# Two-layer graph network on one core: a gather ring of 35 groups instead of 11 in layer 0, and the accumulator cleared in two halves between the layers

## The chip, the cores and the metric

The kernel runs on one core of a Trainium2 chip. The metric is the time of one execution on the device in microseconds (us); three executions were timed, and one more was profiled. TensorE, VectorE, ScalarE, GpSimd and SyncE are the core's engines; the profile calls them PE (PEld is TensorE's weight load), DVE, ACT, POOL and SP.

## What is computed

6250 nodes with 128 features, 106250 edges sorted by their destination, 4 edge types. Two layers, each on the normalized features of the one before and added to them:

```python
h = max(layernorm(x), 0)
x = x + segment_sum((h @ W.T + b)[src] * edge_weight[:, None], dst)      # layer 0

h = max(layernorm(x), 0)
msgs = 0
for t in range(4):                                                      # layer 1
    m = relu(concat(h[src], h[dst]) @ W1[t] + b1[t]) @ W2[t] + b2[t]
    msgs = msgs + where(edge_type == t, m, 0)
agg = segment_sum(msgs, dst)
x = x + gru_cell(agg, h)
```

## The kernel before

Edges are taken in tiles of 128 and in groups of `GT` = 4 tiles; there are `NGRP` = 208 groups and 50 chunks of 125 nodes (`NCH`, `CW`). After a prologue (loads, first layernorm, `h @ W.T + b` for all nodes, stored as `h0_tab`) each engine runs its own loop for layer 0 (`f0_pool`, `f0_act`, `f0_pe`, `f0_dve`, `f0_sp`) and then for layer 1 (`f1_...`). The order on each engine is the order in which these loops are written; engines meet only at semaphores.

Layer 0, for group g:

- GpSimd (`f0_pool`, line 1164) issues four indirect DMAs, each of which gathers the 128 source rows of one tile from `h0_tab` into a slot of a ring, `slot0(g % R0)`. The ring has `R0` = 11 slots of 4 x 132 columns of the array `accs`. From group 11 on it waits until `out0` is at least g - R0 + 1, that is, until TensorE has done with the group that was in the slot.
- ScalarE (`f0_act`, `weigh`, line 1253) waits for the four transfers and multiplies each row by its edge weight in place. It is 4 groups ahead of the step of the loop.
- VectorE (`f0_dve`, `hots`, lines 1182 and 1183) writes the one-hot matrices of the edge's node in the chunk and of its type. It is 6 groups ahead, in a ring of `HR` = 8, and waits for `out0` of at least g - 7.
- TensorE (`f0_pe`, `group`, line 1311) multiplies the two and sums two groups into a PSUM bank; eight passes are recorded per group. It counts up `out0`.
- VectorE (`gather_sums`, line 1223) adds the finished sums of two groups to the nodes in `xs`, after a wait for `out0` of at least 2(o + 1) for pair o.

For each chunk c whose sums are complete, some groups later: VectorE computes the layernorm (`variance`, `normalize`, lines 1191 to 1207), TensorE transposes it (`turned`, lines 1319 and 1320), ScalarE applies the relu (`hidden`, line 1268), TensorE multiplies with the two halves of `W1` (lines 1326 and 1333), ScalarE and VectorE copy the results out (`p_out`, line 1274; `q_out`, line 1212), and SyncE stores them as `p_tab` and `q_tab` (lines 1355 and 1357). `st` has one place for each, so `q_out` waits for the store before.

Layer 1 uses the same array `accs` (25088 columns) as its accumulator and needs it zero. Its lower half (12544 columns, up to `A0`) holds the one-hot ring and the gather ring in layer 0, its upper half only prologue data. So ScalarE clears the upper half in 50 pieces, one after each `p_out` (`clear`, line 1278), two unused pieces at step 0, and, when all groups are done, the rest in 12 pieces (`zero`, line 1247). VectorE waits for `zeroed` = R0 + 3 and `c_zero` = 50 before its first accumulation of layer 1.

At the start of layer 1, GpSimd (line 1369) gathers from `p_tab` as soon as all groups of layer 0 and all stores of `p_tab` are done, into a ring of 12 groups. VectorE writes three one-hot matrices (`hots`, line 1411), TensorE transposes them (line 1520), ScalarE copies the transposes (`hot_copy`, line 1473), TensorE expands the rows of `q_tab` (line 1529), VectorE adds the gathered rows (`total`, line 1419, which frees a slot), ScalarE applies the relu (line 1477), TensorE sums (line 1539), VectorE accumulates (line 1464).

Of the kernel before, what the change touches and what calls it, by code (L numbers as in the profile page):

```python
# [27 lines left out]
ACT = mybir.ActivationFunctionType  # L28
AX = mybir.AxisListType.X

P = 128
WIN = 32
GT = 4
# [4 lines left out]
CW = 125  # L38
# [6 lines left out]
def gnn_program(nc, x, src, dst, etype, eweight, W0, b0, W1, b1, W2, b2, Wih, Whh, bih, bhh, out):  # L45
    N, D = x.shape
    E = src.shape[0]
    T = W1.shape[0]
    KEYS = WIN * T
    NCH = N // CW  # L50
# [4 lines left out]
    PB = NT // PR // NBLK  # L55
    NCOL = NT + UT
    NW = -(-N // WIN)
    NPAD = NW * WIN
# [16 lines left out]
    with ExitStack() as ctx:  # L75
        def sb(name, shape, dt=F32):
            return ctx.enter_context(nc.sbuf_tensor(name, shape, dt))
# [5 lines left out]
        accs = sb("accs", [P, NPAD * T])  # L83
        acc0 = accs[:, 0:NPAD]
        cnt = accs[0:T + 1, NPAD:2 * NPAD]
        A0 = 2 * NPAD
# [28 lines left out]
        nought = sb("nought", [P, 1])  # L115
# [47 lines left out]
        LIN = NCH * D  # L163
        x_rows = accs[0:CW, 0:LIN].rearrange("p (c d) -> p c d", d=D)
        TG = [(c, min(4, NCH - c)) for c in range(0, NCH, 4)]
# [11 lines left out]
        g_cnt = cntb[:, 0, :]  # L177

        NGRP = NT // GT
        R0, R1 = 11, 12  # L180
        FW = D + T
        HR = 8
        NOCT = NT // (NBLK * PR)
        GO = NGRP // NOCT
        F0 = LIN
        assert NOCT == PB and F0 + R0 * GT * FW <= A0 and F0 + (len(TG) - 1) * 4 * D <= A0 and HR * GT * CW <= LIN
        from_t = nodehot[0:CW, :, :, :].rearrange("p a b n -> p (a b n)")[:, 0:NOCT]
        next_t = nodehot[0:CW, :, :, :].rearrange("p a b n -> p (a b n)")[:, NOCT:2 * NOCT]

# [6 lines left out]
        def slot1(k):  # L196
# [33 lines left out]

            "mid_d mid_a mid_p st_c st_h st_p st_q upd_d upd_a upd_p upd_ld upd_st "

            "iota_set c_var c_sqrt c_nrm c_hT c_h1 c_p c_pe c_q c_qe c_zero "

            "u_agg u_aggc u_gate u_rz u_pre u_tanh u_new u_out u_add").split()}
        s_x = [sem(f"s_x{i}") for i in range(NPC)]
# [414 lines left out]
        def h0_stored(eng):  # L651
            eng.wait_ge(s["tab"], 32 * len(TG))
# [517 lines left out]
        def f0_dve(eng):  # L1170
# [38 lines left out]
            def q_out(c):  # L1209
                eng.wait_ge(s["c_q"], c + 1)  # L1210
                eng.wait_ge(s["st_q"], c * 16 + 16)
                eng.tensor_tensor(st[0:CW, 2, :], pb[5][0:CW, :], b1r[0:CW, :], ALU.add).then_inc(s["c_qe"], 1)
# [13 lines left out]
            for g in range(-SEEN0, STEPS0):  # L1226
                if g + SEEN0 < NGRP:
                    hots(g + SEEN0)
                o = (g - GO) // GO
                if (g - GO) % GO == 0 and 0 <= o < NOCT:  # L1230
                    if o % 4 == 0:
                        first = bases(eng, NT // PR + o, 4, NCH - 1)
                    gather_sums(o, first[o % 4])
                if (c := chunk_at(g, D_NRM)) is not None:
                    normalize(c)
                if (c := chunk_at(g, D_STATS)) is not None:
                    variance(c)
                if (c := chunk_at(g, D_Q)) is not None:
                    q_out(c)

        def f0_act(eng):
            h0_stored(eng)
            eng.wait_ge(s["preT"], 6)
            ZW = -(-(NPAD * T - A0) // NCH)

            def zero(ap):
                eng.activation(ap, nought[0:ap.shape[0], :].to_broadcast([ap.shape[0], ap.shape[1]]), ACT.Copy).then_inc(s["zeroed"], 1)

            def weigh(g):
                G0 = slot0(g % R0)  # L1250
                eng.wait_ge(s_g0[g % R0], 16 * GT * (g // R0 + 1))
                for t in range(GT):
                    ins = eng.activation(G0[:, t, 0:D], G0[:, t, 0:D], ACT.Copy, scale=w_t[:, g * GT + t:g * GT + t + 1])  # L1253
                ins.then_inc(s["dv0"], 1)

            def root(c):
                eng.wait_ge(s["c_var"], c + 1)
                if c >= 2:
                    eng.wait_ge(s["c_nrm"], c - 1)
                eng.activation(sd2[0:CW, c % 2, :], mv2[0:CW, c % 2, 1:2], ACT.Sqrt).then_inc(s["c_sqrt"], 1)  # L1260

            def hidden(c):
                eng.wait_ge(s["c_hT"], c + 1)
                if c >= 2:
                    eng.wait_ge(s["c_q"], c - 1)
                eng.wait_ge(s["st_h"], max(c, 1) * 16)
                eng.wait_ge(s["st_c"], max(c, 1) * 16)
                eng.activation(h1b[:, c % 2, :], pb[4][:, 0:CW], ACT.Relu, scale=2.0)  # L1268
                eng.activation(cntb[0:T, c % 2, :], pb[4][0:T, 128:128 + CW], ACT.Copy).then_inc(s["c_h1"], 1)

            def p_out(c):
                eng.wait_ge(s["c_p"], c + 1)
                eng.wait_ge(s["st_p"], c * 16 + 16)
                eng.activation(st[0:CW, 1, :], pb[7][0:CW, :], ACT.Copy).then_inc(s["c_pe"], 1)

            def clear(c):
                part_c = accs[:, A0 + c * ZW:min(A0 + (c + 1) * ZW, NPAD * T)]
                eng.activation(part_c, nought[:, :].to_broadcast([P, part_c.shape[1]]), ACT.Copy).then_inc(s["c_zero"], 1)

            for g in range(-WEIGHED0, STEPS0):  # L1280
                if g + WEIGHED0 < NGRP:
                    weigh(g + WEIGHED0)
                if (c := chunk_at(g, A_HID)) is not None:
                    hidden(c)
                if (c := chunk_at(g, A_ROOT)) is not None:
                    root(c)
                if (c := chunk_at(g, A_P)) is not None:
                    p_out(c)
                    clear(c)
                if g == 0:  # L1290
                    zero(accs[:, HR * GT * CW:LIN])
                    zero(accs[:, F0 + R0 * GT * FW:A0])
            eng.wait_ge(s["out0"], NGRP)
            zero(accs[:, 0:HR * GT * CW])
            for k in range(R0):
                zero(accs[:, F0 + k * GT * FW:F0 + (k + 1) * GT * FW])

        def f0_pe(eng):
            eng.wait_ge(s["preC"], 6)
# [104 lines left out]
        def f1_dve(eng):  # L1404
# [37 lines left out]
            for g in range(-3, STEPS1):  # L1442
                if g + 3 < NGRP:
                    hots(g + 3)
                if 0 <= g + 1 < NGRP:
                    total(g + 1)
                if (c := chunk_at(g, 4)) is not None:
                    add_x(c)
                if (c := chunk_at(g, 2)) is not None:
                    candidate(c)  # L1450
                if (c := chunk_at(g, 3)) is not None:
                    blend(c)
                if 0 <= g < NGRP:
                    if g == 0:
                        eng.wait_ge(s["zeroed"], R0 + 3)
                        eng.wait_ge(s["c_zero"], NCH)
                    if g % NG == 0:
                        base = bases(eng, g * GP, NG * GP)
                    eng.wait_ge(s["out1"], g + 1)
                    for p in range(GP):  # L1460
                        if g or p:
                            eng.wait_ge(s["acc1"], g * GP + p)
                        a = accs[:, bass.ds(base[g % NG * GP + p] * T, KEYS)]
                        eng.tensor_tensor(a, pb[4 + g % 2][:, p * KEYS:(p + 1) * KEYS], a, ALU.add).then_inc(s["acc1"], 1)  # L1464
# [228 lines left out]
```

## Time and profile before

| | us |
|---|---|
| median of 3 executions | 2747.63 (2742.65 to 2761.39) |
| the profiled execution | 2750.62 |
| its span | 2748.6 |
| first and last gather of layer 0 issued | 67.6 and 1259.5 |
| last `q_out` of layer 0 | 1300.8 |
| GpSimd busy | 1592.7 (58%) |
| TensorE busy | 1388.9 (51%) |
| VectorE busy | 799.1 (29%) |
| ScalarE busy | 637.3 (23%) |

The span is the profiled execution as its instructions show it; 2 us lie around it. Issuing an indirect DMA counts as busy time of GpSimd. No engine is busy for two thirds of the span, so the time is in who waits for whom.

### The profile page before, as it was taken

The numbers are of one execution on the slowest core, as the hardware profiler recorded it, in microseconds if no ns is written. First come the engines' busy times: TensorE is split into PE (matmuls) and PEld (weight loads), VectorE is DVE, ScalarE is ACT, GpSimd is POOL, SyncE is SP. The second block draws the span as 40 slices with busy tenths as digits, with TensorE's granted clock in tenths as the row PEclk, the third lists the DMA queues.
The fourth block names the chain that finished last, engine by engine and source line by source line (L and its number), as shares of the span: only waits on it lengthen the run. The fifth ranks groups of instructions, "written<-read, shape, count | busy, mean of one in ns | idle before, by whom it ended". The sixth has DMA issues, their size and how long they took to land.

```text
span 2748.6 us, 25831 instructions
## 1 busy us (share of the span) xinstructions
PE 1388.9 (51%) x7484; PEld 1186.3 (43%) x7484; DVE 799.1 (29%) x2307; ACT 637.3 (23%) x1773; POOL 1592.7 (58%) x1697
## 2 busy tenths in 40 slices
PE   4233444344344444444146555665655656666666
PEld 3222333233233323332145555555555655555556
DVE  6112222222222222223023233333323333333333
ACT  4212222222222222223011212121212122122122
POOL 2756666666666666662755555555555555555550
PEclk9556666566566656666578888888888798888889
DMA  8212222222222222222222222222222222222220
GB/s 190 53 40 54 75 70 73 67 72 75 68 70 76 71 67 69 79 71 77 66 58 60 61 69 58 67 60 67 62 67 60 67 68 62 68 61 67 63 66 24
DMA packets 160437, 186.49 MB, mean 68 GB/s; under 512 B 50285, under 2 KB 118728, under 8 KB 159919
## 3 DMA queue, kind: packets, MB, share of 16 engines
q0 software_dynamic: 53248, 109.16, 15.9%
q1 hardware_dynamic: 105802, 74.84, 9.8%
q8 instruction: 64, 1.05, 0.2%
q10 hardware_dynamic: 1244, 0.79, 0.1%
q14 instruction: 79, 0.65, 0.1%
HBM read 149.29 MB, written 35.35 MB: 67 GB/s over the span
## 4 chain that ended last, share of the span: by engine, by line
another core or an unknown queue 37%; PE 24%; issue 19%; DVE 13%; ACT 2%; SPq 2%; DVEq 2%; DMA 1%; POOL 0%; ACTq 0%
PE bank L1539 6%; PE bank L1529 5%; PE bank L1311 4%; PE bank L1520 4%; DVE hot L1411 2%; DVE accs L1464 2%; DVE accs L1183 2%; DVE xs L1223 1%; DVE rows L1419 1%; SPq L313 1%; ACT hotT L1473 1%; PE bank L1552 1%; DMA q_tab<-st 1%; DVEq L701 1%
## 5 line engine op out<-in xcount | busy, mean ns | idle before, releaser
L1164 POOL DMA_INDIRECT accs<-h_tab,src_t x832 | 787.4, 946 | 433.8 <-issue 239.5
L1311 PE MATMUL bank<-accs 128*125 128x132 f32 x1664 | 374.7, 360 | 414.8 <-issue 387.6
L1311 PEld LDWEIGHTS bank<-accs 128*125 128x125 f32 x1664 | 329.8, 264 | 518.6 <-issue 499.1
L1520 PE MATMUL bank<-ident,hot 128*128 128x128 f32 x832 | 166.5, 334 | 597.7 <-DVE hot L1411 388.5
L1369 POOL DMA_INDIRECT G<-p_tab,src_t x288 | 272.4, 946 | 259.1 <-DVE rows L1419 129.6
L1464 DVE TENSOR_TENSOR accs<-bank,accs 128x128 f32 x416 | 121.3, 292 | 924.3 <-remote 376.6
L1520 PEld LDWEIGHTS bank<-ident,hot 128*128 128x128 f32 x832 | 107.6, 166 | 637.1 <-DVE hot L1411 409.1
L1369 POOL DMA_INDIRECT edge<-p_tab,src_t x272 | 257.3, 946 | 190.5 <-DVE rows L1419 106.4
L1529 PE MATMUL bank<-qwin,hotT 128*128 128x128 f32 x1664 | 288.7, 331 | 0.9 <-ACT hotT L1473 0.9
L1253 ACT ACTIVATE accs<-accs,edge 128x128 f32<-128x128 f32 x832 | 258.2, 387 | 96.7 <-DMA accs<-h_tab,src_t 96.7
L1539 PE MATMUL bank<-hot,rows 128*128 128x128 f32 x1664 | 272.8, 318 | 1.2 <-ACT rows L1477 1.2
L1529 PEld LDWEIGHTS bank<-qwin,hotT 128*128 128x128 f32 x1664 | 269.7, 245 | 1.0 <-ACT hotT L1473 1.0
L1539 PEld LDWEIGHTS bank<-hot,rows 128*128 128x128 f32 x1664 | 259.6, 237 | 1.6 <-ACT rows L1477 1.6
L1223 DVE SCALAR_TENSOR_TENSOR xs<-bank,nodehot,xs 125x132 f32 x208 | 64.0, 349 | 455.7 <-remote 309.8
L1473 ACT ACTIVATE hotT<-bank 128x512 f32<-128x512 f32 x208 | 123.8, 595 | 283.4 <-PE bank L1520 165.8
L1369 POOL DMA_INDIRECT g_more<-p_tab,src_t x136 | 128.6, 946 | 77.5 <-issue 44.3
L1319 PE MATMUL bank<-ident,st 125*128 125x125 f32 x50 | 21.1, 421 | 290.7 <-DVE st L1207 191.2
L1268 ACT ACTIVATE h1b<-bank 128x125 f32<-128x125 f32 x50 | 13.8, 276 | 642.7 <-remote 519.7
L1182 DVE TENSOR_TENSOR accs<-bank,edge 128x16 f32<-128x16 f32 x208 | 36.5, 176 | 420.8 <-remote 334.2
L1483 ACT ACTIVATE st<-bank 128x125 f32<-128x125 f32 x50 | 13.9, 277 | 583.6 <-remote 312.7
L1319 PEld LDWEIGHTS bank<-ident,st 125*128 125x128 f32 x50 | 8.5, 170 | 309.3 <-DVE st L1207 205.8
L1411 DVE TENSOR_TENSOR hot<-bank,key_t 128x512 f32<-128x512 f32 x208 | 141.4, 681 | 0.1
(158 smaller groups left out, 1734.0 us busy)
## 6 DMA issues: line engine op xcount, KB each, us to landing
qwin<-q_tab SPq DMA_DIRECT2D x416, 64.0 KB
accs<-h_tab,src_t POOLq DMA_INDIRECT x832
q_tab<-st SPq DMA_DIRECT2D x50, 250.0 KB
p_tab<-st SPq DMA_DIRECT2D x49, 250.0 KB
G<-p_tab,src_t POOLq DMA_INDIRECT x288
edge<-p_tab,src_t POOLq DMA_INDIRECT x272
h_tab<-h1b SPq DMA_DIRECT2D x50, 62.5 KB
h1b<-h_tab SPq DMA_DIRECT2D x50, 62.5 KB
```

Of the source, the lines that this page charges most:

```text
L1164: eng.indirect_dma_start(slot0(g % R0)[:, t, 0:D], None, h0_tab, bass.IndirectOffsetOnAxis(src_t[:, k:k + 1], 0)).then_inc(s_g0[g % R0], 16)
L1183: eng.tensor_tensor(ones_of(g % HR), mid(iota_p[:, 0:CW], GT), bcast(rel_t[:, cols], CW), ALU.is_equal).then_inc(s["hot0"], 1)
L1223: ins = eng.scalar_tensor_tensor(a, got, m[:, o:o + 1], a, ALU.mult, ALU.add)
L1253: ins = eng.activation(G0[:, t, 0:D], G0[:, t, 0:D], ACT.Copy, scale=w_t[:, g * GT + t:g * GT + t + 1])
L1311: ins = eng.matmul(pb[SUM_BANK[o % 4]][0:CW, 0:FW], ones_of(g % HR)[:, t, :], slot0(g % R0)[:, t, :], start=n == 0, stop=n == GO * GT - 1)
L1369: eng.indirect_dma_start(slot1(g % R1)[:, t, :], None, p_rows, bass.IndirectOffsetOnAxis(src4_t[:, k:k + 1], 0)).then_inc(s_g1[g % R1], 16)
L1411: eng.tensor_tensor(hot[:, g % NG], mid(iota_p, GT), bcast(key_t[:, g * GT:(g + 1) * GT], KEYS), ALU.is_equal).then_inc(s["hot1"], 1)
L1464: eng.tensor_tensor(a, pb[4 + g % 2][:, p * KEYS:(p + 1) * KEYS], a, ALU.add).then_inc(s["acc1"], 1)
L1473: eng.activation(hotT[:, g % 2, :], pb[0][:, :], ACT.Copy).then_inc(s["tc1"], 1)
L1520: ins = eng.transpose(pb[0][:, t * P:(t + 1) * P], hot[:, g % NG, t, :], ident[:, :])
L1529: ins = eng.matmul(pb[2 + g % 2][:, t * D:(t + 1) * D], hotT[:, g % 2, t * P:(t + 1) * P], qwin[:, g % NG, t // PR, :], start=True, stop=True)
L1539: ins = eng.matmul(pb[4 + g % 2][:, p * KEYS:(p + 1) * KEYS], rows[:, g % 2, t, :], hot[:, g % NG, t, :], start=t % PR == 0, stop=t % PR = ...
```

## The change

The ring of layer 0 becomes 35 slots. It begins where it began (`F0` = 6400) and now ends at column 24880, in the upper half of `accs`. The 50 clears within layer 0 and the 14 other clears of ScalarE go. In their place VectorE clears the upper half in one memset after its last `q_out`, and ScalarE the lower half in one activation after `out0` = 208. `zeroed` is now waited for at 2. The number of gather semaphores follows R0.

```diff
-        R0, R1 = 11, 12
+        R0, R1 = 35, 12
...
-        assert NOCT == PB and F0 + R0 * GT * FW <= A0 and ...
+        assert NOCT == PB and F0 + R0 * GT * FW <= NPAD * T and ...
...
                 if (c := chunk_at(g, D_Q)) is not None:
                     q_out(c)
+            eng.memset(accs[:, A0:], 0.0).then_inc(s["zeroed"], 1)
...
                 if (c := chunk_at(g, A_P)) is not None:
                     p_out(c)
-                    clear(c)
-                if g == 0:
-                    zero(accs[:, HR * GT * CW:LIN])
-                    zero(accs[:, F0 + R0 * GT * FW:A0])
             eng.wait_ge(s["out0"], NGRP)
-            zero(accs[:, 0:HR * GT * CW])
-            for k in range(R0):
-                zero(accs[:, F0 + k * GT * FW:F0 + (k + 1) * GT * FW])
+            eng.activation(accs[:, 0:A0], nought[:, :].to_broadcast([P, A0]), ACT.Copy).then_inc(s["zeroed"], 1)
...
                     if g == 0:
-                        eng.wait_ge(s["zeroed"], R0 + 3)
-                        eng.wait_ge(s["c_zero"], NCH)
+                        eng.wait_ge(s["zeroed"], 2)
```

On GpSimd, at the start of layer 0 (`h_tab` is the gathered table, `s_out0` TensorE's count of finished groups), before:

```order
L678 COMPARE_AND_BRANCH
L1590 UNCONDITIONAL_BRANCH
L1164 DMA accs<-h_tab,src_t 128x128 [waits s_preC,s_preT,s_tab]
L1164 DMA accs<-h_tab,src_t 128x128 x43
L1164 DMA accs<-h_tab,src_t 128x128 [waits s_out0]
L1164 DMA accs<-h_tab,src_t 128x128 x3
```

and now:

```order
L678 COMPARE_AND_BRANCH
L1575 UNCONDITIONAL_BRANCH
L1164 DMA accs<-h_tab,src_t 128x128 [waits s_preC,s_preT,s_tab]
L1164 DMA accs<-h_tab,src_t 128x128 x139
L1164 DMA accs<-h_tab,src_t 128x128 [waits s_out0]
L1164 DMA accs<-h_tab,src_t 128x128 x3
```

The first wait for TensorE stands ahead of gather 141 instead of 45 (counted from 1).

On ScalarE, at the end of layer 0 (`nought` is the zero that is copied), before:

```order
L1274 ACTIVATE st<-bank 125x512 [waits s_st_p,s_c_p]
L1278 ACTIVATE accs<-nought 128x245
L1247 ACTIVATE accs<-nought 128x4000 [waits s_out0]
L1247 ACTIVATE accs<-nought 128x528 x11
L1467 ACT_TABLE_LOAD
L1467 ACTIVATE tiny<-tiny 128x1
L1473 ACTIVATE hotT<-bank 128x512 [waits s_tr1] x2
```

and now:

```order
L1270 ACTIVATE st<-bank 125x512 [waits s_st_p,s_c_p] x2
L1282 ACTIVATE accs<-nought 128x12544 [waits s_out0]
L1452 ACT_TABLE_LOAD
L1452 ACTIVATE tiny<-tiny 128x1
L1458 ACTIVATE hotT<-bank 128x512 [waits s_tr1] x2
```

Twelve clears ahead of the table load have become one, of 12544 columns in place of 9808.

On VectorE, at the same place, before:

```order
L1207 TENSOR_SCALAR st<-xs,mv,rs 125x128 [waits s_c_hT,s_step]
L1212 TENSOR_TENSOR st<-bank,b1r 125x512 [waits s_st_q,s_c_q] x3
L561 TENSOR_TENSOR brz<-bg 128x2 [waits s_sets,s_tab]
L1411 TENSOR_TENSOR hot<-bank,key_t 128x512 x3
L1419 TENSOR_TENSOR rows<-bank,G 128x512 [waits s_gather1_0,s_exp1]
```

and now:

```order
L1207 TENSOR_SCALAR st<-xs,mv,rs 125x128 [waits s_c_hT,s_step]
L1212 TENSOR_TENSOR st<-bank,b1r 125x512 [waits s_st_q,s_c_q] x3
L1240 MEMSET accs 128x12544
L561 TENSOR_TENSOR brz<-bg 128x2 [waits s_sets,s_tab]
L1397 TENSOR_TENSOR hot<-bank,key_t 128x512 x3
L1405 TENSOR_TENSOR rows<-bank,G 128x512 [waits s_gather1_0,s_exp1]
```

The memset stands between the last `q_out` of layer 0 and the first one-hot matrices of layer 1.

## Rows read from the trace of the kernel before

**Rows 1.** The page's groups: busy, mean ns of one | idle time before, releaser.

```profile
L1164 POOL DMA_INDIRECT accs<-h_tab,src_t x832 | 787.4, 946 | 433.8 <-issue 239.5
```

**Rows 2.** Lines 1164 and 1253 until 330 us, 1164 after it; 1253 in the page.

```profile
L1164 POOL DMA_INDIRECT accs<-h_tab,src_t x186: 942/947/1183, 67.6 to 329.5; - x186
...
L1164 POOL DMA_INDIRECT accs<-h_tab,src_t x647: 942/947/973, 329.5 to 1259.5; - x162
...
  remote: 114.3, 37
  PE bank L1311: 20.7, 7
...
L1253 ACT ACTIVATE accs<-accs,edge 128x128 f32<-128x128 f32 x832 | 258.2, 387 | 96.7 <-DMA accs<-h_tab,src_t 96.7
...
L1253 ACT ACTIVATE accs<-accs,edge x176: 384/386/402, 74.2 to 327.5; 128x128 f32<-128x128 f32 x176
...
  DMA accs<-h_tab,src_t: 96.7, 21
```

**Rows 3.** Timeline, 104 to 180 us: start, us, engine, what, [idle before <-releaser].

```profile
116.50 0.62 DVE L1223 SCALAR_TENSOR_TENSOR xs<-bank,nodehot,xs 125x132 f32 x2 [21.86 <-remote]
...
126.19 0.38 PE L1311 MATMUL bank<-accs 128*125 128x132 f32 x1 [2.41 <-issue]
...
138.87 0.17 DVE L1182 TENSOR_TENSOR accs<-bank,edge 128x16 f32<-128x16 f32 x1 [21.08 <-remote]
...
157.81 7.00 PE L1311 MATMUL bank<-accs 128*125 128x132 f32 x38 [0.35 <-issue]
157.91 0.62 DVE L1223 SCALAR_TENSOR_TENSOR xs<-bank,nodehot,xs 125x132 f32 x2 [18.28 <-remote]
158.03 0.95 POOL L1164 DMA_INDIRECT accs<-h_tab,src_t  x1 [10.43 <-remote]
```

**Rows 4.** Timeline of GpSimd in the middle of layer 0.

```profile
333.28 0.94 POOL L1164 DMA_INDIRECT accs<-h_tab,src_t  x1 [0.30 <-issue]
...
347.04 0.94 POOL L1164 DMA_INDIRECT accs<-h_tab,src_t  x1 [4.06 <-remote]
...
375.84 0.95 POOL L1164 DMA_INDIRECT accs<-h_tab,src_t  x1 [4.08 <-PE bank L1311]
...
1032.61 0.95 POOL L1164 DMA_INDIRECT accs<-h_tab,src_t  x1 [3.99 <-remote]
```

**Rows 5.** Timeline of GpSimd and VectorE at the start of layer 1.

```profile
1302.57 0.95 POOL L1369 DMA_INDIRECT G<-p_tab,src_t  x1 [42.12 <-DMA p_tab<-st]
...
1381.54 0.29 DVE L1464 TENSOR_TENSOR accs<-bank,accs 128x128 f32 x1 [43.62 <-remote]
...
1383.74 0.95 POOL L1369 DMA_INDIRECT G<-p_tab,src_t  x1 [11.45 <-DVE rows L1419]
```

**Rows 6.** End of layer 0: line 1311 in a stretch (PE and PEld busy, passes), line 1212.

```profile
1259.50 0.95 POOL L1164 DMA_INDIRECT accs<-h_tab,src_t  x1 [0.31 <-issue]
...
1262.70:1277.60 14.90, 9.09 (x64) 8.98 (x64) 0.81 0.25 76
...
L1212 DVE TENSOR_TENSOR st<-bank,b1r x7: 681/692/692, 1264.9 to 1300.8; 125x512 f32<-125x512 f32 x7
```

**Rows 7.** Timeline: memsets of the prologue, ScalarE and VectorE between the layers; two forms.

```profile
3.23 0.91 DVE L487 MEMSET accs<- 8x1024 int32 x1 [0.16 <-issue]
4.31 0.91 DVE L488 MEMSET accs<- 8x1024 f32 x1 [0.16 <-issue]
...
L1247 ACT ACTIVATE accs<-nought 128x528 f32<-128x528 f32 x11 | 5.9, 628 | 0.0
...
L1247 ACT ACTIVATE accs<-nought 128x4000 f32<-128x4000 f32 x1 | 3.5, 3526 | 0.0
...
1298.01 9.37 ACT L1247 ACTIVATE accs<-nought 128x4000 f32<-128x4000 f32 x12
...
1308.80 0.58 ACT L1473 ACTIVATE hotT<-bank 128x512 f32<-128x512 f32 x1
...
1312.53 0.69 DVE L1419 TENSOR_TENSOR rows<-bank,G 128x512 f32<-128x512 f32 x1 [9.13 <-issue]
```

More of the change, by code:

```diff
@@ L185, in gnn_program @@
         F0 = LIN
-        assert NOCT == PB and F0 + R0 * GT * FW <= A0 and F0 + (len(TG) - 1) * 4 * D <= A0 and HR * GT * CW <= LIN
+        assert NOCT == PB and F0 + R0 * GT * FW <= NPAD * T and F0 + (len(TG) - 1) * 4 * D <= A0 and HR * GT * CW <= LIN
         from_t = nodehot[0:CW, :, :, :].rearrange("p a b n -> p (a b n)")[:, 0:NOCT]
@@ L231, in gnn_program @@
             "mid_d mid_a mid_p st_c st_h st_p st_q upd_d upd_a upd_p upd_ld upd_st "
-            "iota_set c_var c_sqrt c_nrm c_hT c_h1 c_p c_pe c_q c_qe c_zero "
+            "iota_set c_var c_sqrt c_nrm c_hT c_h1 c_p c_pe c_q c_qe "
             "u_agg u_aggc u_gate u_rz u_pre u_tanh u_new u_out u_add").split()}
@@ L1243, in f0_act @@
             eng.wait_ge(s["preT"], 6)
-            ZW = -(-(NPAD * T - A0) // NCH)
-            def zero(ap):
-                eng.activation(ap, nought[0:ap.shape[0], :].to_broadcast([ap.shape[0], ap.shape[1]]), ACT.Copy).then_inc(s["zeroed"], 1)
             def weigh(g):
@@ L1274, in p_out @@
                 eng.activation(st[0:CW, 1, :], pb[7][0:CW, :], ACT.Copy).then_inc(s["c_pe"], 1)
-            def clear(c):
-                part_c = accs[:, A0 + c * ZW:min(A0 + (c + 1) * ZW, NPAD * T)]
-                eng.activation(part_c, nought[:, :].to_broadcast([P, part_c.shape[1]]), ACT.Copy).then_inc(s["c_zero"], 1)
             for g in range(-WEIGHED0, STEPS0):
```

## The prediction

> **What bounds the kernel now.** I read the groups of the page first, for who waits in layer 0. GpSimd is the busiest engine there: 832 gathers of 946 ns, and 433.8 us idle in front of them [rows 1]. That looks like a gather-bound layer whose ring is too short. So I next asked what ended those waits, and where. Between 330 and 1262 us (647 gathers) 37 waits of 114.3 us ended by a "remote" semaphore and 7 of 20.7 us by TensorE, 135.0 us together [rows 2]. In this stretch that can only be the ring wait on `out0` (the rest, "issue", is the 0.30 us between two gathers). A ring that is full means that the producer is ahead. The other side says the same: ScalarE, which takes each group when it has landed, waited for gathers 96.7 us in the whole run, and all 96.7 us lie before 330 us [rows 2]. After that every group had landed when it was asked for. The consumers set the pace, and a gather issued earlier helps nobody at that moment.
>
> Why do the consumers crawl, when TensorE does eight groups in 14.9 us once the gathers have ended [rows 6]? The timeline of the first gathers answers [rows 3]. GpSimd issues without a pause from 67.6 (rows 2) to 147.6 us (158.03 - 10.43). VectorE waits for `out0` = 4 until 116.50, for 5 (21.08 us of it in one wait) until 138.87 and for 6 until 157.91 (wait values read from `hots` and `gather_sums`): 22.4 us, then 19.0 us, for a group of eight passes, 2.8 us per pass, though the passes are issued no earlier than their data is there and nothing else is waited for ("issue"). Then, 10.4 us after the last gather of the run was issued, everything moves: TensorE does 38 passes in 7.0 us and the ring opens (GpSimd [10.43 <-remote]). The same happens at the start of layer 1: gathers run from 1302.6 to 1372.3 (1383.74 - 11.45), VectorE waits 43.62 us until 1381.54, and the ring opens after 11.45 us [rows 5]. In the steady state it is a short cycle: 20 gathers, then a stop of 4 us until TensorE's count arrives. It was 4.06 us at 347.04, 4.08 us at 375.84 (28.8 us later, so a run of 24.7 us, which is 20 gathers of 1.25) and 3.99 us at 1032.61 [rows 4]. I read this as a coupling: while gathers are issued back to back, TensorE's completions trickle, and a pause of the gathers releases them. About 38 passes (nearly five groups) of backlog are released at each pause, and that is why the cycle is five groups in 28.8 us, 5.76 us per group. What the coupling consists of the profile does not show.
>
> **The trace against a rule.** By rows 3 and 5 TensorE's counts arrive only when GpSimd's gathers pause. The Trainium skill ("SBUF — State Buffer", section "Who interferes with whom") says the opposite: TensorE and ScalarE have their own ports, never wait on anyone, and a DMA never contends with a compute engine. By that rule the slow passes are TensorE's own and a longer uninterrupted run of gathers costs nothing. What it would make of the time is rival B, worked out there from rows. The trace does not agree so far; it does not exclude it either, as no stretch without gathers and with the same work lies before 1260 us.
>
> **The change, part by part.** The sum is made on the profiled execution (2750.62 us, span 2748.6); the median of the runs shown, 2747.63, is 3.0 us lower, which is taken off at the end.
>
> (a) *GpSimd's head start.* With 35 slots the first ring wait stands before gather 141 instead of 45, and it passes if `out0` is 1. A gather costs 0.947 + 0.30 = 1.25 us, a group 5.01 us. At TensorE's 22.4 us per group, `out0` is 5 at 138.9 and grows by one each 22.4 us. Group 47 needs `out0` = 13, due near 318 us, while GpSimd would be there at 67.6 + 47 x 5.01 = 303.1 us; group 46 needs 12 at 298.1, which is just there. So the first full ring comes at group 47 at 303 us, and ends with the release after about 11 us (10.43 and 11.45 are the two releases after long runs), at 314 us. Before, group 47 was issued at 333.28 us [rows 4] (gather 186 at 329.5, rows 2). Gain: **-19 us**. Bounds: if the release grows with the run (10.43 us after 80 us, so 0.13 x 235 = 31 us), nothing is gained, 0; if TensorE trickles at 11.5 us per group, as it does inside the short cycles, the ring fills near group 58 and the gain is about -33 us.
>
> (b) *The remaining 161 groups.* One slot is freed per group in either kernel, so the ring is full as before and the cycle of 20 gathers and a 4 us stop stays: 0 us. GpSimd's last gather ended at 1259.5 + 0.95 = 1260.4 us [rows 6] and now ends at 1241 us.
>
> (c) *The backlog at the end.* When GpSimd ends its last gather, TensorE is a ring behind: about 34 groups in place of 10, 24 more. They are worked off without gathers beside them. The rate: 64 passes, eight groups, in 14.9 us, 1.86 us a group; and the last seven `q_out` stand 35.9 / 6 = 5.98 us apart, 1.50 us per group, set by the store of `q_tab` before each [rows 6]. Between these I take 1.7 us: **+41 us** (bounds +36 and +45). Thus (a) and (c) put the end of layer 0, which was the end of the last `q_out` at 1300.8 + 0.7 = 1301.5, at 1301.5 - 19 + 41 = 1324 us.
>
> (d) *The clears.* VectorE's new memset of 12544 columns lies behind its last `q_out` and ahead of layer 1's first `hots`. The four prologue memsets of 1024 columns start 1.07 us apart [rows 7], so it takes 12544 x 1.07 / 1024 = 13.1 us. ScalarE's last clears took 9.37 us for 9808 columns; one of 12544 takes, by the 4000-column row (3.53 us, 0.83 ns a column above the fixed part), 10.7 us, +1.3 us, and stays hidden behind VectorE's. The first `total` of layer 1 was at 1312.53, after ScalarE's clears and table load (first copy at 1308.80) [rows 7]. Now it is 13.1 us of memset plus about 5 us of hots, transposes, copy and expansion after 1301.5, so 1319.6: 7 us later against the start of the layer. But GpSimd's gathers start at once, and the ring of 12 fills 60 us later, with TensorE trickling meanwhile; its release decides when work moves, and there group 14 waits for `total(2)`. I count about one handshake, **+3 us** (bounds 0 and +13, the whole memset). The 50 clears of 0.4 us inside layer 0 lay in ScalarE's waits; their removal counts 0.
>
> Sum: -19 + 0 + 41 + 3 = +25 us, 2775.6 us profiled, **2772 us** as a median. That is 0.9% over before; about 1% is what a measurement of this kernel can tell from no change, so the forecast is "same, at its slow edge". With the bounds of (a), (c) and (d), half of each taken, its own range is 2755 to 2792.
>
> **The rivals.**
> - *A, the release grows with the run (slower).* One mechanism: the pause that frees TensorE is proportional to the gathers issued before it. For it: 10.43 us after 80 us, 4.06 after 24.7. Against it: 11.45 us after only 70 us [rows 4, 5], which looks like a fixed backlog. It decides once a run is over some 150 us. The first stop costs 31 us instead of 11, (a) is 0: 2747.6 + 0 + 41 + 3 = 2792 us.
> - *B, no coupling (same).* TensorE is slow by itself and the gathers are innocent. For it: the passes are also spaced out in places where ScalarE and VectorE idle; against it: the release a constant 4 us after each stop, and fast passes everywhere after 1262. Then `out0` = 208 comes at 1277.6 as before, the gathers merely wait in the slots, and only (d) with 3 to 13 us remains: 2755 us.
> - *C, the ring was the bound (faster).* GpSimd never stops: 67.6 + 208 x 5.01 = 1110 us, the tail of 41 us behind it gives 1151 instead of 1301.6, minus 151 us, plus 3: 2600 us. For it: the 135 us of ring waits; against it: not one wait of ScalarE for a gather after 330 us.
> - *D, the memset holds up the first gathers of layer 1.* It begins at the moment at which GpSimd issues them (1302.57, rows 5). If they queue behind it, layer 1 starts 12 us later on top: 2784 us. For it: no memset of VectorE lies beside a gather in the trace, so nothing excludes it; against it: of 647 gathers beside VectorE's other work none took over 0.973 us, where the median is 0.947 [rows 2].
>
> **How the numbers follow.** Forecast 0.50, A 0.17, B 0.20, C 0.06, D 0.07. Slower by over 1% (above 2775): all of A, most of D and about 0.2 of the forecast, 0.43. Faster by over 1%: C and a little of a lucky start, 0.08. Within 1%: 0.49. The range reaches down past B to 2742 and up past A, whose backlog could drain at 1.86 us a group, to 2805.
>
> **What would show it.** Right: GpSimd issues some 188 gathers without a stop, until about 303 us; the first stop is 10 to 12 us; then the cycle of 20 gathers and 4 us; the last gather near 1241 us; 40 us more between it and the end of layer 0; TensorE's `out0` waits on VectorE of 22 us until after 300 us. The memset 13.1 us, and the first `total` 18 us after the last `q_out`. Wrong: a first stop of 30 us (A); TensorE keeping its old pace with gathers long finished and a full set of slots (B); gathers ending near 1110 us and the layer with them (C); the first gather of layer 1 held back behind the memset (D). If TensorE completes groups at less than 11 us each during the long first run, the step from rows 3 fails.

## The result and the profile after

| | before | changed |
|---|---|---|
| median of the timed runs, us | 2750.53 (4 runs, 2742.65 to 2761.39) | 2783.62 (4 runs, 2769.98 to 2796.91) |
| ratio to before, 95% interval | 1 | 1.0109 (1.0059 to 1.0159) |
| profiled execution, us (span) | 2750.62 (2748.6) | 2779.37 (2777.3) |

The changed kernel is slower by 1.1%, 30 us (0.6 to 1.6%; the two medians are 33 us apart). The interval lies wholly above a ratio of 1, but the difference is small, and the runs of the two kernels spread over 19 and 27 us. The forecast was 2772 us, +0.9%. In the changed kernel the gather stays at line 1164; ScalarE's weighing is line 1249, the group's passes line 1297, the memset line 1240, ScalarE's one clear line 1282, the gathers of layer 1 line 1355 and their sums line 1405.

The page and the view of the gather's line, to be held against [rows 1, 2] (idle time before, and what ended it):

```profile
span 2777.3 us, 25768 instructions
...
L1164 POOL DMA_INDIRECT accs<-h_tab,src_t x832 | 787.2, 946 | 425.6 <-issue 241.6
```

```profile
L1164 POOL DMA_INDIRECT accs<-h_tab,src_t x832: 938/944/1237, 68.8 to 1251.8; - x167
...
  remote: 124.6, 32
  PE bank L1297: 30.6, 10
...
  ACT accs L1249: 78.9, 18
```

The ring waits are still there: 155 us in 42 waits, against 166 us in 51 before. ("remote" is a wait whose end has no record in the trace; at this line only TensorE's count `out0` can end one.) Tripling the ring removed next to nothing of them, because the ring fills once and then opens at the consumers' pace. ScalarE waits 78.9 us for gathers (96.7 before), so the producer is still ahead.

Now the first stretch, from timelines of the changed kernel (start, us, engine, what, [idle before <-releaser]). PE is TensorE's matmul, PEld its weight load. First TensorE alone, then VectorE alone:

```profile
91.76 2.10 PE L1297 MATMUL bank<-accs 128*125 128x132 f32 x8 [2.90 <-issue]
...
106.73 2.09 PE L1297 MATMUL bank<-accs 128*125 128x132 f32 x8 [2.87 <-issue]
111.67 1.65 PE L1297 MATMUL bank<-accs 128*125 128x132 f32 x6 [2.84 <-issue]
114.60 0.38 PE L1297 MATMUL bank<-accs 128*125 128x132 f32 x1 [1.28 <-issue]
```

```profile
92.90 0.17 DVE L1182 TENSOR_TENSOR accs<-bank,edge 128x16 f32<-128x16 f32 x1 [7.64 <-remote]
...
115.98 0.17 DVE L1182 TENSOR_TENSOR accs<-bank,edge 128x16 f32<-128x16 f32 x1
...
137.75 0.17 DVE L1182 TENSOR_TENSOR accs<-bank,edge 128x16 f32<-128x16 f32 x1 [21.03 <-issue]
```

For the first 44 us of gathers TensorE is not slow: from 76.96 to 113 us it starts eight passes in 2.1 us, one group each 5 us, as fast as the gathers bring them. What is late is its count. VectorE's three operations above wait for `out0` = 3, 4 and 5. The last passes of these groups end by the record (ends are modelled) at 88.9, 93.9 and 98.9 us, and the operations start 4, 22 and 39 us later. For the eighth group the delay is 87 us, and there it stays up to the 13th: about four groups are run and not yet counted. Only when the delay has grown this far, from 113 us on, do the passes themselves start late. The other three traces with these times (before, e11, e12) show the same in the same order. In short, "TensorE creeps" below means: a count of `out0` each 22.4 us, and from 113 us on a pass each 2.8 us.

Then rows from the stretch up to the release, from timelines of all engines:

```profile
204.23 0.29 PEld L1297 LDWEIGHTS bank<-accs 128*125 128x125 f32 x1 [2.51 <-issue]
...
206.33 0.38 PE L1297 MATMUL bank<-accs 128*125 128x132 f32 x1 [3.12 <-issue]
...
208.43 0.28 PEld L1297 LDWEIGHTS bank<-accs 128*125 128x125 f32 x1 [3.91 <-issue]
209.14 0.38 PE L1297 MATMUL bank<-accs 128*125 128x132 f32 x1 [2.43 <-issue]
...
210.54 0.28 PEld L1297 LDWEIGHTS bank<-accs 128*125 128x125 f32 x1 [1.83 <-issue]
...
211.93 0.38 PE L1297 MATMUL bank<-accs 128*125 128x132 f32 x1 [2.41 <-issue]
...
316.48 0.94 POOL L1164 DMA_INDIRECT accs<-h_tab,src_t  x1 [10.21 <-remote]
...
318.33 0.38 PE L1297 MATMUL bank<-accs 128*125 128x132 f32 x1 [3.12 <-issue]
...
335.37 0.94 POOL L1164 DMA_INDIRECT accs<-h_tab,src_t  x1 [14.21 <-remote]
...
342.86 3.27 PE L1297 MATMUL bank<-accs 128*125 128x132 f32 x12 [0.32 <-issue]
343.82 0.94 POOL L1164 DMA_INDIRECT accs<-h_tab,src_t  x1 [3.76 <-remote]
```

GpSimd ran from 68.8 us almost without a stop to 306.3 us (316.48 - 10.21): 188 gathers, as forecast. From 113 us on a weight load and its matmul started mostly 1.4 or 2.1 us apart, 2.8 us per pass, as in [rows 3]. The `hots` of VectorE, which wait for one count each, start at 181.8, 204.9, 226.6, 249.7, 271.4, 294.5 and 316.2 us: 22.4 us each. But the stop of 10.2 us brought no release; at 318 us TensorE still crept. GpSimd got one slot, did one group, stopped for 14.2 us, did one more, stopped for 3.8 us, and only then (342.86: twelve passes in 3.27 us) was TensorE free. So TensorE crept for 37 us in which GpSimd issued only eight gathers. From 384 us on the old cycle runs: gathers for 24.7 us, a stop of 4.0 us.

The end of layer 0 and the start of layer 1 in the changed kernel: the last `q_out` additions in the view of line 1212, then the timeline.

```profile
L1212 DVE TENSOR_TENSOR st<-bank,b1r x50: 679/683/692, 399.5 to 1328.0; 125x512 f32<-125x512 f32 x50
```

```profile
1326.04 10.65 ACT L1282 ACTIVATE accs<-nought 128x12544 f32<-128x12544 f32 x1
...
1327.99 0.69 DVE L1212 TENSOR_TENSOR st<-bank,b1r 125x512 f32<-125x512 f32 x1 [4.03 <-DMA q_tab<-st]
...
1329.73 0.94 POOL L1355 DMA_INDIRECT G<-p_tab,src_t  x1 [77.01 <-DMA p_tab<-st]
1330.98 0.94 POOL L1355 DMA_INDIRECT G<-p_tab,src_t  x1 [0.30 <-issue]
1331.25 10.51 DVE L1240 MEMSET accs<- 128x12544 f32 x1 [2.56 <-issue]
...
1341.69 1.88 DVE L1397 TENSOR_TENSOR hot<-bank,key_t 128x512 f32<-128x512 f32 x3
...
1351.43 0.69 DVE L1405 TENSOR_TENSOR rows<-bank,G 128x512 f32<-128x512 f32 x1 [7.86 <-remote]
...
1410.62 0.94 POOL L1355 DMA_INDIRECT G<-p_tab,src_t  x1 [11.29 <-DVE rows L1405]
```

GpSimd's one long wait between the layers, 42.12 us in [rows 5], is now 77.01 us. This is the loss. The stages of the two profiled executions side by side, in us:

| | before | changed | difference |
|---|---|---|---|
| last gather of layer 0 ends | 1260.4 | 1252.7 | -7.7 |
| first gather of layer 1 starts | 1302.6 | 1329.7 | +27.2 |
| last gather of layer 1 starts | 2673.7 | 2701.4 | +27.7 |
| span | 2748.6 | 2777.3 | +28.7 |

The head start is worth 7.7 us, the longer backlog costs 34.9 us, and what comes after it (the clears among it) 0.5 us up to the last gather and 1.0 us more behind it. The backlog can be counted: when GpSimd's last gather of layer 0 ended, TensorE had started the passes of 200 of the 208 groups before, and of 176 now. These 24 groups are the 24 added slots. They arise in the first run: at 347 us, with GpSimd at group 49 in either kernel, TensorE had started 42 groups before and 20 now. They are worked off fast, with no gathers beside them; the view of line 1297 up to 1300 us:

```profile
L1297 PE MATMUL bank<-accs x221: 274/276/428, 1258.8 to 1300.0; 128*125 128x132 f32 x111
```

221 passes in 41.2 us are 1.5 us per group.

### The profile page after: what moved, and what is told of

It is laid out like the page before. It is cut to its first block, busy times and chain, and to the rows that moved or that the text cites. A ratio compares the mean times of both kernels' runs of the same rounds, so it can differ in the third digit from the quotient of the medians.

```text
span 2777.3 us, 25768 instructions
## 1 busy us (share of the span) xinstructions
PE 1370.3 (49%) x7484; PEld 1172.8 (42%) x7484; DVE 808.2 (29%) x2308; ACT 619.9 (22%) x1710; POOL 1590.4 (57%) x1697
## 4 chain that ended last, share of the span: by engine, by line
another core or an unknown queue 40%; PE 23%; issue 17%; DVE 12%; ACT 3%; SPq 2%; DMA 2%; DVEq 1%; ACTq 0%
PE bank L1514 5%; PE bank L1524 5%; PE bank L1297 4%; PE bank L1505 4%; DVE hot L1397 2%; DVE accs L1449 2%; DVE accs L1183 2%; DVE rows L1405 1%; ACT accs L1249 1%; DVE xs L1223 1%; SPq L313 1%; PE bank L1537 1%; ACT hotT L1458 1%; DMA q_tab<-st 1%
## 5 line engine op out<-in xcount | busy, mean ns | idle before, releaser
L1297 PE MATMUL bank<-accs 128*125 128x132 f32 x1664 | 364.7, 350 | 491.0 <-issue 466.9
L1297 PEld LDWEIGHTS bank<-accs 128*125 128x125 f32 x1664 | 319.9, 254 | 594.3 <-issue 582.3
L1249 ACT ACTIVATE accs<-accs,edge 128x128 f32<-128x128 f32 x832 | 257.9, 387 | 78.9 <-DMA accs<-h_tab,src_t 78.9
L1183 DVE TENSOR_TENSOR accs<-bank,edge 128x500 f32<-128x500 f32 x208 | 139.2, 669 | 0.0
```

What stands on the lines that cost most here:

```text
L1183: eng.tensor_tensor(ones_of(g % HR), mid(iota_p[:, 0:CW], GT), bcast(rel_t[:, cols], CW), ALU.is_equal).then_inc(s["hot0"], 1)
L1297: ins = eng.matmul(pb[SUM_BANK[o % 4]][0:CW, 0:FW], ones_of(g % HR)[:, t, :], slot0(g % R0)[:, t, :], start=n == 0, stop=n == GO * GT - 1)
```

## The experiments

One fact has to be known to read them. The first ten runs fell on chips (two of them) on which the kernel before takes about 2200 us, not 2750: one fifth less for the same program. The last two fell on a chip of the 2750 us kind. "Kind" says only this; whether it is the chip or a state that it was in, no run shows. Each run stands beside the kernel before, on its own chip, so the ratios are sound, but they answer for that kind of chip.

**e1_clears_only**: the changed kernel, with the ring put back.

```diff
-        R0, R1 = 35, 12
+        R0, R1 = 11, 12
```

> The new clears alone, with the old ring of 11. My theory (gathers issued back to back hold up TensorE's completions; the long ring costs 24 more groups of backlog, the clears almost nothing): 0 to +4 us against the kernel before (ratio 1.000 to 1.0015), layer 0's last q_out near 1301 us as before, the first total of layer 1 some 20 us after it, but the last gather of layer 1 within 3 us of before. Rival (the clears cost it: the memset of 13.1 us stands on the path at the start of layer 1): +13 us or more, ratio 1.005 and up.

Measured: 2201.42 us against 2201.23, ratio 0.9999 (0.999 to 1.0008). The gathers end at 1107 us and never wait for the ring. The clears cost nothing, here.

**e2_slots35_waits11**: the changed kernel, 35 slots, but GpSimd waits as if there were 11.

```diff
-                if g >= R0:
-                    eng.wait_ge(s["out0"], g - R0 + 1)
+                if g >= 11:
+                    eng.wait_ge(s["out0"], g - 11 + 1)
```

> 35 slots, but the gather of group g waits for out0 of g - 10 as with 11 slots; everything else as changed. My theory: what counts is how far GpSimd may run ahead, not where the slots lie: the same as e1_clears_only within 3 us, first stop of the gathers at group 16 near 148 us, cycle of 20 gathers and 4 us. Rival (the cost comes with the slots themselves, their place in the array or the number of semaphores): like the changed kernel, +25 to +35 us.

Measured: 2200.8 us, ratio 1.0 (0.9991 to 1.0009). As no gather waits for the ring on this kind of chip, this does not tell how far GpSimd may run ahead from the slots themselves, and the run was not made on the other kind.

**e3_ring23**: the changed kernel with 23 slots (`R0, R1 = 23, 12`).

> Ring of 23, half way. My theory: the first stop comes at group 31 near 223 us, 10 us of head start are won over the kernel before, 12 more groups of backlog at 1.5 to 1.7 us cost 18 to 20 us: +10 to +15 us in all, half of the changed kernel's. Rival (a threshold: a ring above some size is slow at once, or a cost of the clears): the same as the changed kernel, +25 us or more; or 0.

Measured: 2199.75 us, ratio 0.9996 (0.9987 to 1.0005). Nothing costs anything on this chip, the ring neither. The reason is plain in the profile of e5, below.

**e4_gathers_stop_at_35**: the changed kernel, in which the gathers of groups 35 to 207 of layer 0 are left out; those groups are computed on the rows that lie in the slots. It no longer computes the layer; it shows what the consumers can do with no gathers beside them.

```diff
-            for g in range(NGRP):
-                if g >= R0:
-                    eng.wait_ge(s["out0"], g - R0 + 1)
+            for g in range(R0):
...
-                eng.wait_ge(s_g0[g % R0], 16 * GT * (g // R0 + 1))
+                eng.wait_ge(s_g0[g % R0], 16 * GT)
```

> The changed kernel, in which GpSimd gathers only the first 35 groups of layer 0 and all later groups work on what then lies in the slots (the gathers of 173 groups are left out). It tells the coupling from rival B. My theory: from the last gather near 245 us plus about 10 us on, TensorE's counts come at once and the consumers do a group in 1.5 to 1.9 us: layer 0's last q_out near 255 + 200 x 1.6 + 24 = 570 to 650 us. Rival B (TensorE is slow by itself, 5.7 us per group whether gathers run or not): layer 0 still ends near 1300 us.

Measured: 1593.86 us (one run). A row of the view of stretches (stretch, length, then busy time of PE, PEld, DVE, ACT and POOL, granted clock, DMA share, GB/s):

```profile
260.00:400.00 140.00, 133.12 (x878) 105.49 (x877) 131.74 (x463) 132.03 (x468) 0.00 (x0) 1.00 0.31 97
```

738 of the 878 passes are those of the groups (the others belong to the chunks), 92 groups in 140 us, with TensorE, VectorE and ScalarE all over 90% busy and the granted clock at its full 2.4 GHz: 1.5 us per group. The last `q_out` starts at 531 us, ahead of the 570 to 650 expected. The consumers need a third of GpSimd's 5.0 us per group. This is a chip of the 2200 us kind, so the run does not decide against rival B for the other; there the 1.5 us per group after the last gather, shown above, says the same of the work itself.

**e5_changed_again**: the changed kernel, unaltered, on a second chip of the 2200 us kind.

> The changed kernel once more. On the chip of the last four runs the kernel before took 2201 us instead of 2750, and its gathers never stopped. My theory now has a condition: the long ring costs only where TensorE's completions trickle while gathers run. So where the kernel before takes about 2200 us, this one is the same within 3 us (ratio 0.999 to 1.002), layer 0's last gather at 1107 us; where it takes about 2750 us, the ratio is 1.008 to 1.014 again. Rival (the change is slower by its instructions alone): 1.005 or more in both.

Measured: 2203.3 us against 2203.8, ratio 0.9994 (0.9984 to 1.0003). The view of the gather's line there:

```profile
L1164 POOL DMA_INDIRECT accs<-h_tab,src_t x832: 941/946/1181, 68.1 to 1108.0; - x167
...
  issue: 243.3, 798
...
  PE bank L1297: 10.1, 33
...
  ACT accs L1249: 752.0, 163
```

and its timeline at the place where the 2750 us chip shows a pass each 2.8 us:

```profile
206.12 1.75 PE L1297 MATMUL bank<-accs 128*125 128x132 f32 x8 [2.98 <-issue]
...
211.15 2.09 PE L1297 MATMUL bank<-accs 128*125 128x132 f32 x8 [3.28 <-ACT accs L1249]
```

The gathers themselves are as fast (946 ns, 0.30 us apart). But eight passes take 1.75 us, not 22.4, and each count of `out0` is seen within 2 us of the group's last pass. GpSimd never stops, ScalarE waits 752 us for gathers, and the layer is bound by the gathers' issue. It is the picture that rival C drew, with its number (last gather near 1110 us), but with either ring: on such a chip 11 slots are more than enough, and 35 change nothing.

**e6_pause_after_gathers**: the kernel before, with a memset of 128 columns on GpSimd, waited for, after each gather of layer 0.

```diff
+                    pool_seq(eng, eng.memset(rest[:, :], 0.0))
```

> The kernel before (ring 11), with a GpSimd memset of 128 columns, and a wait for it, after each gather of layer 0: 0.2 to 0.4 us more per gather, so 1.5 to 1.65 us instead of 1.25. Where gathers never stop (2200 us), the layer is as long as its gathers: 832 x 0.3 = +170 to +330 us. Where TensorE's completions trickle (2750 us), my theory is that the back-to-back issue is what holds them up: spaced gathers free them and the stops of 4 us vanish, so the layer grows by no more than 832 x 1.6 - 1193 = +140 us and may even be unchanged. Rival (TensorE slow by itself there): stops stay, time unchanged within 5 us.

Measured: 2372.98 us, ratio 1.0764 (1.0743 to 1.0786). The gathers come each 1.44 us and end at 1281.7. The 169 us more are 832 gathers at 0.2 us each, just below the range that was expected. Without the trouble, pauses are pure loss. Whether they would pay on the other kind was not tried.

**e7_packets_ring11** and **e8_packets_ring35**: the kernel before and the changed one, with small loads added to each chunk, to see whether crowded DMA engines make TensorE creep.

```diff
+                for i in range(2):
+                    if c:
+                        eng.wait_ge(s_rest[i], 16 * c)
+                    with nc.allow_non_contiguous_dma(reason="small packets"):
+                        eng.dma_start(rest[:, i, :, 0:8], h0_tab[i * P:(i + 1) * P, :].rearrange("p (a b) -> p a b", b=8)).then_inc(s_rest[i], 16)
```

> The kernel before, with two extra loads per chunk in layer 0, each of 2048 descriptors of 32 bytes, into a scratch tile that nothing reads, issued by SyncE. It asks whether a stream of small packets can bring about the trickle of TensorE's completions on a chip where the kernel before takes 2201 us. My theory (too many small packets in flight hold up TensorE's completions): GpSimd shows ring waits, TensorE's passes spread to over 1 us with nothing waited for, the layer gets over 50 us longer. Rival (the trickle belongs to the chip on which the first runs were made and packets do not matter): layer 0 ends within 15 us of 1137 us, no ring waits.

> The same extra loads in the changed kernel (ring of 35). If the packets bring the trickle about: slower than e7_packets_ring11 by 10 to 30 us, as the backlog at the end of the gathers is 24 groups larger. If they only slow the gathers or nothing: the same as e7_packets_ring11 within 4 us. If the longer ring absorbs late gathers (my rival C): faster than e7.

Measured: 2206.29 us, ratio 1.0026 (1.0014 to 1.0038), and 2204.88 us, 1.0027 (1.0015 to 1.0039), with 366838 packets in place of 160437. Over twice the packets, no ring wait and no late count: on this kind of chip such packets don't bring the trickle about. The same on a chip that has it was not run.

**e9_slow_consumer_ring11** and **e10_slow_consumer_ring35**: the kernel before and the changed one, with 48 redundant products per pair of groups, so that TensorE is slow by its own work at any time, gathers or not.

```diff
+                for i in range(48 if g % GO == 0 else 0):
+                    eng.matmul(pb[SUM_BANK[o % 4]][0:CW, 0:FW], ones_of(g % HR)[:, i % GT, :], slot0(g % R0)[:, i % GT, :],
+                               start=True, stop=True)
```

> The kernel before with 48 additional products per pair of groups in layer 0, whose result the next product overwrites, so that TensorE by itself needs 6 to 8 us a group, more than the 5.0 us of its gathers. It makes a consumer that is slow whether gathers run or not, which is what rival B took the first traces for. Expected of both theories: GpSimd shows ring waits from about group 12 to 40 on, layer 0 takes 208 x 6 to 8 us, 200 to 500 us more than 2201 us.

> The same additional products in the changed kernel (ring of 35). With a consumer that is merely slow, the length of the ring decides only when gathers are issued, not when groups are finished: the same as e9 within 4 us (ratio to e9 0.998 to 1.002). If that holds, a slow consumer alone does not explain the +1.1% of the first comparison, and what is needed is a consumer that is slow only while gathers run, with a backlog at their end. Rival (a long ring costs whenever consumers are behind): e10 slower than e9 by 15 us or more.

Measured: 2562.83 us, ratio 1.1639 (1.162 to 1.1659), and 2559.93 us, 1.1631 (1.1612 to 1.165). The view of the gather's line, first with 11 slots, then with 35:

```profile
L1164 POOL DMA_INDIRECT accs<-h_tab,src_t x832: 938/944/1180, 71.8 to 1416.5; - x167
...
  PE bank L1314: 333.5, 87
```

```profile
L1164 POOL DMA_INDIRECT accs<-h_tab,src_t x832: 938/944/1180, 67.0 to 1249.2; - x167
...
  PE bank L1300: 158.1, 45
```

With 35 slots the gathers end 167 us earlier, and the consumers finish at nearly the same time: the last `q_out` starts at 1500.3 us with 11 slots and at 1495.8 with 35. So a consumer that is merely slow makes the ring's length indifferent, as was expected (within 4 us). A loss by the ring needs something else: a consumer whose lateness depends on the gathers. That is the difference between rival B and the forecast.

**e11_clears_only_again**: e1 once more, now on a chip of the 2750 us kind.

> The changed kernel with its ring put back to 11 slots, once more, because all runs so far fell on chips on which the gathers never stop. If the kernel before takes about 2750 us beside it: the coupling theory with the cost in the backlog gives 2750 + 0 to 3 us (ratio 1.000 to 1.002), a last gather of layer 0 near 1260 us and a last q_out near 1301 us. The rival, that the clears hold up layer 1, gives 2770 or more with the last q_out still at 1301. If the kernel before takes about 2200 us, the ratio is 1.000 again and it tells nothing new.

Measured: 2754.76 us (10 runs) against 2750.68 (19 runs), ratio 1.0019 (0.9989 to 1.005). Last gather of layer 0 ends at 1261.1 us, last `q_out` starts at 1295.8 (near 1260 and 1301 were expected). The measured +5 us is above the 0 to 3 of the coupling theory, but its interval (-3 to +14 us) holds them and ends below the changed kernel's 1.0059: the clears alone are not what costs 1.1%. Its timeline around the first stop:

```profile
158.24 0.94 POOL L1164 DMA_INDIRECT accs<-h_tab,src_t  x1 [8.13 <-remote]
...
165.99 0.95 POOL L1164 DMA_INDIRECT accs<-h_tab,src_t  x1 [3.08 <-remote]
```

**e12_ring23_again**: e3 once more, on the same chip as e11.

> The changed kernel with 23 slots, once more. If the kernel before takes about 2750 us beside it: backlog of 22 groups instead of 10, so about half of the cost, 12 groups x 1.5 us = +18, less a head start of 4 to 8, ratio 1.003 to 1.006, last q_out near 1312 us. A cost that comes from any long first run of gathers alone would be the full 1.011. If the kernel before takes about 2200 us, the ratio is 1.000 again.

Measured: 2767.06 us (10 runs), ratio 1.0049 (1.0013 to 1.0084). Last gather ends at 1254.7 us, last `q_out` starts at 1304.5 (1312 was expected). The ratio is the one that was expected, and its interval excludes the 1.011 of a cost that any long first run brings. The timeline around its first stops:

```profile
228.93 0.94 POOL L1164 DMA_INDIRECT accs<-h_tab,src_t  x1 [6.15 <-remote]
...
245.73 0.94 POOL L1164 DMA_INDIRECT accs<-h_tab,src_t  x1 [12.11 <-remote]
...
253.50 0.94 POOL L1164 DMA_INDIRECT accs<-h_tab,src_t  x1 [3.10 <-remote]
```

With 11, 23 and 35 slots and the same clears the ratios are 1.0019, 1.0049 and 1.0109: the cost grows with the ring. The intervals of neighbours overlap; those of 11 and 35 slots do not (up to 1.005, from 1.0059). The third was taken at another time, but the trend agrees with the traces. In GpSimd's wait between the layers (end of the last gather to the first of layer 1) the step shows by itself: 36.5, 51.4 and 77.0 us.

The four traces of the 2750 us kind also tell how long TensorE needs to come free. All stops up to the release are added, and set against the gathering before them:

| kernel | slots | gathering until the release, us | stops until the release, us | share |
|---|---|---|---|---|
| before | 11 | 80.0 | 10.4 | 0.13 |
| e11 | 11 | 84.6 | 8.1 + 3.1 = 11.2 | 0.13 |
| e12 | 23 | 164 | 6.2 + 12.1 + 3.1 = 21.4 | 0.13 |
| changed | 35 | 247 | 10.2 + 14.2 + 3.8 = 28.2 | 0.11 |

The pause that frees TensorE is not fixed. It grows with the gathers that ran before it, about one us for each eight or nine, over a threefold range. (In the steady cycle it is 4.0 us for 24.7, 0.16, and at the start of layer 1 11.45 us for 69.7, 0.16, so the share falls somewhat as the run grows.)

## Why the prediction came out as it did

The size and the sign of the total were right: 2772 us forecast and 2784 measured, +0.9% and +1.1%. The place was right too: the loss stands between the last gather and the end of layer 0. That the sum came so close is in part luck: against the traces (a) is off by +11.3 us, (c) by -6.1 and (d) by -2.5, which leaves +2.7. By its own steps:

- *What bounds layer 0* (ring waits that are the consumers' pace, not a short ring): right for this kind of chip. The waits went only from 166 us to 155 with three times the slots, and ScalarE waited less for gathers than before. The reading of [rows 3], passes of 2.8 us each, is true only from about 113 us on. In the kernel before, too, the first seven groups run at eight passes in 2.1 us (75.63 to 107.7 us), and what is late from the third on is the count. The forecast worked from the counts, so its sum stands.
- *(a) The head start*, forecast -19 us by a first stop of 11 us. The run was as drawn (188 gathers, to 306.3 us against 303 forecast, a count each 22.4 us). The stop was not: "ends with the release after about 11 us" failed. Two releases after runs of 80 and 70 us had been read as a fixed backlog; in truth the pause grows with the run, and it took 28 us. This is rival A's mechanism, whose chance was put at 0.17. It had priced the pause at 31 us and the head start at 0. GpSimd came to group 49 at 343.8 us against 347.04 in [rows 4], -3.2 us. By its last gather the lead was -7.7 us; where the other 4.5 us come from was not looked into. The later pair has about the same: -6.4 us with 23 slots (1254.7 against 1261.1 in e11). The fault lay in the weighing of two rows against one: 11.45 us after 70 us of gathers was held to refute A, while it lies as near to A's line (9 us) as to a constant.
- *(b) The cycle* of 24.7 us and a stop of 4 us, unchanged: right, it runs from 384 us on.
- *(c) The backlog*, +41 us for 24 groups at 1.7 us: measured 77.0 - 42.1 = +34.9 us, 1.45 us per group, just below the lower bound of 36; against e11, which has the same clears, it is 77.0 - 36.5 = +40.5 us, or 1.69 per group. The two kernels with 11 slots differ by 5.6 us here, so the number is no better known than that; that it depends on the point of the cycle at which the gathers end is a guess. Mechanism and number of groups (24) were right, the size within this spread. Layer 0 ended at 1328.7 us (last `q_out`), forecast 1324: (a) gave 11 us less, (c) took 6 less.
- *(d) The clears*, +3 us: at most +0.5 us up to the last gather in the traces, and 1.0019 (-3 to +14 us) by e11. The memset took 10.5 us, not 13.1. The first `total` of layer 1 comes 22.7 us after the end of the last `q_out` (18 forecast, 11 before). But GpSimd feels nothing of it: its first ring wait of layer 1 is 11.29 us, 11.45 before. The memset is hidden behind the gathers, as the forecast had it.
- *Rival B*, TensorE slow by itself, at 2755 us: the traces stand against it, where eight passes take 2.1 us beside the first gathers and a group 1.5 us after the last. So does the measured loss: e9 with e10 show, if on the other kind, that steady slowness leaves the ring free of cost. *Rival C*: wrong on this kind of chip, true of the other kind for both kernels. *Rival D*: no gather was held back beside the memset; two gathers at 1329.73 and 1330.98 us, just ahead of it, are 1.25 us apart, and the eight issued while it ran keep that distance. It falls.

The rule named beside the first rows was from the Trainium skill ("SBUF — State Buffer", section "Who interferes with whom"): TensorE waits on nobody for its port and a DMA never contends with compute. On the chips of the 2200 us kind the trace agrees (eight passes in 1.75 us with gathers issued back to back). On the 2750 us kind it agrees for the first 44 us of gathers (eight passes in 2.1 us); after that the same passes take 22.4 us. As the counts are late before the passes are, this need not be a matter of ports at all; no run here shows what it is, nor what sets the two kinds apart.

Shown on the 2750 us kind: TensorE's counts fall behind while gathers are issued back to back, then its passes too, and both come free in pauses that grow with the gathers before them; the loss grows with the ring, as a backlog of as many groups as slots were added; the clears are at most a minor part. Shown only on the 2200 us kind: steady slowness of the consumer and added packets don't do it. Argued and not shown: that the gathers cause the lateness. It builds up with them, outlasts them and is gone after a pause, as a queue would be that they fill, but no run tried to switch it off on a chip that has it. e4 (no gathers) and e6 (pauses) were meant for this and fell on the other kind, as did e2, which tells the place and number of the slots from how far GpSimd may run ahead. No ring tried beats the kernel before: on one kind it is the fastest measured, on the other the rings and clears are all within 0.1%.

## What to carry to other kernels

When a producer's ring waits come from a consumer that is late, a longer ring doesn't buy time: it lets the producer run further ahead, and the whole extra ring is left over as a backlog when the producer ends. With a steadily slow consumer that costs nothing, because the producer ends earlier by as much (e9, e10: 167 us). It costs when the producer does not end earlier (here 7.7 us, for a backlog of 34.9). Before lengthening a ring, multiply the added slots by the consumer's time per slot, and hold that against how much earlier the producer will end. And where two stops in a trace are read as a constant, set each against what ran before it, since a law by which the stop grows fits two such rows as well, and it prices the longer run quite differently. A third rule: when an engine seems slow, compare the times of its instructions with the times at which others see its count. Here the instructions ran at full pace for 44 us beside the gathers, while the fourth count was already about 20 us overdue.

## What had not been expected of the hardware

- The same program takes 2750 us on some chips and 2201 us on others; each repeats within 1.5% on its own (19 runs from 2735 to 2776 us, and 61 from 2195 to 2208). The granted clock differs little (mean 0.73 and 0.79). Gathers take 0.945 us on both.
- On the 2750 us kind TensorE's count is late first: 4, 22 and 39 us for the third to fifth group, up to 87 us, which is four groups, for the eighth to 13th. The first seven groups run at full pace meanwhile. On the 2200 us kind the count is seen within 2 us.
- Once four groups are uncounted, TensorE's instructions start on a coarse beat: the rows at 204.23, 206.33, 208.43, 209.14, 210.54 and 211.93 us are 0.70 us apart or two or three times that. Each instruction then comes late, weight load and matmul alike; the matmul does not take longer (0.38 us).
- The release comes after a pause of 0.11 to 0.16 us per us of gathers, from 25 to 247 us of them.
- A memset of VectorE of 12544 columns of 128 partitions takes 10.5 us, 0.84 ns a column, where 8 partitions of 1024 columns were spaced at 1.07 us. ScalarE's clear of the same width takes 10.65 us, beside it, and neither slows GpSimd's gathers.
